# Two layers of cross-attention on one core: values four units back inside the query projection, scores after six steps, and more low parts on VectorE

## The reference

```python
# layer 0: grouped attention, 32 query heads of 32, 8 key/value heads
q = x @ Wq + bq;  k = ctx @ Wk + bk;  v = ctx @ Wv + bv
attn = softmax(q k^T / sqrt(32) + mask)
out = (attn v) @ Wo + bo
x = layer_norm(out + x) * gamma + beta            # eps 1e-6
# layer 1: 16 heads of 64, keys and values from the normalised context
a = layer_norm(ctx) * gamma1 + beta1              # eps 1e-5
Q = x @ Wq1.T;  K = a @ Wk1.T;  V = a @ Wv1.T
x = x + tanh(gate) * ((softmax(where(mask, Q K^T / 8, -inf)) V) @ Wo1.T)
```

## Time and profile before

| | |
|---|---|
| Median of three runs | 1791.67 us |
| The profiled execution, its own time | 1794.66 us |
| Its span on the core | 1792.8 us |
| PE busy | 1725.7 us, 96% of the span |
| PE weight loads busy | 1432.0 us, 80% |
| VectorE busy | 1149.0 us, 64% |
| GpSimd busy | 1106.7 us, 62% |
| ScalarE busy | 582.1 us, 32% |
| DMA | 278.01 MB, 155 GB/s on average |

### The profile page before, as it was taken

One profiled execution on the slowest core, in us unless ns is written; L12 is line 12 of the kernel. 1 busy time (PEld: TensorE's weight loads), 2 busy tenths in 40 slices (PEclk: granted clock), 3 DMA queues, 4 the chain that ended last, 5 costly groups with the idle time before them and its releaser, 6 DMA issues.

```text
span 1792.8 us, 22372 instructions
## 1 busy us (share of the span) xinstructions
PE 1725.7 (96%) x8449; PEld 1432.0 (80%) x8449; DVE 1149.0 (64%) x1089; ACT 582.1 (32%) x667; POOL 1106.7 (62%) x607
## 2 busy tenths in 40 slices
PE   6899999999999799999999999999999999999998
PEld 5788887888888688888888877788888888888886
DVE  6888888888888566565656555446644664466442
ACT  4444444444445434333433323113311331133110
POOL 2677777777777857565656677436644664466331
PEclk9999999999999999999999999999999999999999
DMA  7433332323225557776777845453744464465432
GB/s 213 115 85 77 102 79 72 83 72 86 72 69 146 159 175 250 222 251 212 254 225 235 284 150 176 144 172 129 224 153 164 144 209 141 165 186 168 140 112 88
DMA packets 277487, 278.01 MB, mean 155 GB/s; under 512 B 62202, under 2 KB 230276, under 8 KB 277380
## 3 DMA queue, kind: packets, MB, share of 16 engines
q1 hardware_dynamic: 275188, 274.49, 49.9%
q10 hardware_dynamic: 2192, 2.10, 0.4%
HBM read 174.77 MB, written 101.71 MB: 154 GB/s over the span
## 4 chain that ended last, share of the span: by engine, by line
PE 58%; DVE 18%; issue 11%; POOL 7%; ACT 6%; DMA 1%; SPq 0%; POOLq 0%; DVEq 0%; ACTq 0%
PE ps L53 18%; PE ps L54 18%; PE ps L55 18%; DVE small L1059 3%; DVE pr L1079 3%; ACT pr L822 3%; DVE pT0r L1092 2%; DVE pT1r L1092 2%; DVE xT0r L990 2%; DVE xT1r L990 2%; ACT ot L816 2%; PE ps L682 1%; PE ps L690 1%; POOL xb L1339 1%; POOL y L1353 1%
## 5 line engine op out<-in xcount | busy, mean ns | idle before, releaser
L1388 POOL TENSOR_TENSOR x2Tl<-x2r,x2Th 128x1024 fp32r<-128x1024 f32 x32 | 76.8, 2400 | 291.9 <-ACT x2Th L931 291.9
L1188 DVE STREAM_TRANSPOSE x2r<-xd 128x1024 f32<-128x1024 f32 x32 | 68.8, 2150 | 211.8 <-PE ps L55 211.8
L1324 POOL TENSOR_TENSOR pr<-pr,small 128x1024 f32<-128x1024 f32 x64 | 122.8, 1919 | 105.0 <-DVE small L1085 105.0
L931 ACT CAST x2Th<-x2r 128x1024 fp32r<-128x1024 f32 x32 | 33.6, 1051 | 376.9 <-DVE x2r L1188 376.9
L1319 POOL TENSOR_TENSOR pr<-pr,small 128x1024 f32<-128x1024 f32 x64 | 123.9, 1936 | 25.5 <-DVE small L1063 25.5
L1059 DVE TENSOR_REDUCE small<-pr 128x16 f32<-128x1024 f32 x64 | 78.0, 1219 | 78.6 <-ACT pr L822 78.6
L1339 POOL TENSOR_TENSOR xb<-xb,bo 128x1024 f32<-128x1024 f32 x32 | 77.8, 2431 | 76.3 <-DMA xb<-in_x_dram 76.3
L1353 POOL TENSOR_TENSOR y<-y,bet 128x1024 f32<-128x1024 f32 x32 | 77.7, 2427 | 52.4 <-DVE y L1104 52.4
L53 PE MATMUL ps<-wo0h,oc1l 128*128 128x512 f32 x256 | 102.6, 401 | 3.6 <-DVE y L1143 3.6
L1104 DVE TENSOR_TENSOR y<-y,gam 128x1024 f32<-128x1024 f32 x32 | 54.6, 1706 | 80.0 <-ACT y L856 80.0
L53 PE MATMUL ps<-wo0h,oc0l 128*128 128x512 f32 x256 | 102.5, 401 | 2.0 <-DVE wo0l L1014 1.6
(11 more groups left out here) (370 smaller groups left out, 5473.1 us busy)
## 6 DMA issues: line engine op xcount, KB each, us to landing
o_scratch<-ot SPq DMA_DIRECT2D x256, 64.0 KB, 1.8
ocr<-o_scratch SPq DMA_DIRECT2D x16, 1024.0 KB, 7.9
xb<-in_x_dram SPq DMA_DIRECT2D x32, 512.0 KB, 6.8
x_scratch<-y SPq DMA_DIRECT2D x32, 512.0 KB, 5.3
a_scratch<-ost SPq DMA_DIRECT2D x64, 256.0 KB, 3.4
b_scratch<-ost SPq DMA_DIRECT2D x64, 256.0 KB, 5.8
xd<-x_scratch SPq DMA_DIRECT2D x128, 128.0 KB, 2.9
raw<-b_scratch SPq DMA_DIRECT2D x64, 256.0 KB, 5.6
```

The costliest lines, as they stand in the source:

```text
L1324: nc.gpsimd.tensor_tensor(heads(v), heads(v), mx.unsqueeze(2).to_broadcast([P, TPB * GRP, KEYS]), ALU.subtract)\
L1388: nc.gpsimd.tensor_tensor(x2T[1][:], x2r[:], f32(x2T[0][:]), ALU.subtract).then_inc(x2_lo, 1)
```

## The change

**First loads.** SP now issues the context, then Wk, then all four tiles of x; ScalarE issues the two small biases, waits for the context, and then issues Wv and its bias. PE turns the context before it turns the biases, and ScalarE and VectorE split the context before Wk. VectorE makes the low parts of the first four tiles of x; GpSimd made two of them.

**Attention.** In PE's slot u the order is now: four steps of the query projection, the values of unit u-4, two steps, the scores of unit u-1, two steps. ScalarE does the exponential at the head of its slot and `ot` behind the casts. The groups of Wq are split one unit earlier (`wq_groups`), SP's order inside a slot is k, Wq, x, v, and quarter 3 of Wq is issued in slot 1, not before slot 0. The parts of Wo are made one in each slot from 57 to 64. The statistics and the normalised rows of the context are made in slots 12 to 15, stored to a new scratch and loaded again in slot 60. Pieces of the first chunk of `oc` are split two units later.

**Seam.** From h = 53 the low parts of `oc` and all low parts of A of the first batch are on VectorE, and so are the eight of B, `beta` of the last tile, and the low parts of the first and the last probabilities. `coefficients` stands ahead of `residual` on GpSimd there. ScalarE issues the store of the last tile of x2. The pieces of A are loaded and split one in each slot.

```diff
         def wo_groups(u):
-            return (7,) if u == UNITS else (5, 6) if u == UNITS - 1 else (u - (UNITS - 6),) if UNITS - 6 <= u < UNITS else ()
+            return (u - (UNITS - 7),) if UNITS - 7 <= u <= UNITS else ()
+        def wq_groups(u):
+            return (2, 3) if u == 0 else (u + 3,) if u + 3 < KT else ()
...
             load_ctx(ctx, ctx_ld)
-            sp.dma_start(bv_row[:], row(w["bv0"], KV0)).then_inc(b_ld, 16)
-            sp.dma_start(wvr[:], w["Wv0"].rearrange("(k p) n -> p k n", p=P)).then_inc(kv_ld1, 16)
-            load_x(sp, 2)
-            load_x(sp, 3)
+            sp.dma_start(wkr[:], w["Wk0"].rearrange("(k p) n -> p k n", p=P)).then_inc(kv_ld0, 16)
+            for n in range(4):
+                load_x(sp, n)
...
                 if 1 <= u and u + 1 < UNITS:
                     sp.wait_ge(scores, u)
                     load_k(u + 1)
-                if 3 <= u <= UNITS:
-                    sp.wait_ge(pv, u - 2)
-                    load_v(u - 1)
+                if u == 1:
+                    load_wq(3)
...
+                if 4 <= u <= UNITS + 1:
+                    sp.wait_ge(pv, u - 3)
+                    load_v(u - 2)
```

PE's slot:

```diff
                 if u < UNITS:
                     query(range(0, 4))
+                if 4 <= u < UNITS + 4:
+                    values_of(u - 4)
+                if u < UNITS:
+                    query(range(4, 6))
                 if 1 <= u <= UNITS:
                     v = u - 1
...
                 if u < UNITS:
-                    query(range(4, KT))
+                    query(range(6, KT))
...
-                if 3 <= u < UNITS + 3:
-                    v = u - 3
```

ScalarE's and GpSimd's rows at the seam, and VectorE's row:

```diff
+            for c in range(2, 4):
+                split_ab(1, 0, c)
+            act.wait_ge(normed, NTILE)
+            act.dma_start(d["x2"][P * (NTILE - 1):, :], y[(NTILE - 1) % 3][:]).then_inc(y_st[(NTILE - 1) % 3], 16)
+            for c in range(4, KT):
                 split_ab(1, 0, c)
...
             total(1)
+            prob_lo(0)
             gamma(NTILE - 1)
-            for c in range(1, KT, 2):
+            dve.wait_ge(scaled, NTILE)
+            nc.vector.tensor_tensor(y[(NTILE - 1) % 3][:], y[(NTILE - 1) % 3][:], bet0[:], ALU.add).then_inc(normed, 1)
+            for c in range(KT):
                 low(1, 0, c)
...
             turn_prob(NTILE - 1)
+            prob_lo(NTILE - 1)
             finish(NTILE - 2)
...
-                if half == 1 and n + 1 < NTILE:
+                seam = h > LEAD + TAB * KT
+                if half == 1 and n + 1 < NTILE and not seam:
                     residual(n + 1)
...
                 if half == 1:
                     coefficients(n)
-                if later:
+                if seam and half == 1 and n + 1 < NTILE:
+                    residual(n + 1)
+                if later and not seam:
                     chunk_lo(h // 4 + 1, 1)
```

More of the change, by code:

```diff
@@ L606, in query, with values_of @@
                         last.then_inc(q_done, 1)
+                def values_of(v):
+                    pe.wait_ge(p_lo, v + 1)
+                    pe.wait_ge(v_ld[v % 2], 16 * 4 * (v // 2 + 1))
+                    after(pe, o_ev, v - 1)
+                    for c in range(2):
+                        last = three(nc, V[v % 2], [vb[v % 2][:, c, x] for x in (0, 1)], [pT[v % 2][x][:, c].rearrange("p j n -> p (j n)") for x in (0, 1)],
+                                     c == 0, c == 1)
+                    last.then_inc(pv, 1)
                 if u < UNITS:
                     query(range(0, 4))
+                if 4 <= u < UNITS + 4:
+                    values_of(u - 4)
+                if u < UNITS:
+                    query(range(4, 6))
                 if 1 <= u <= UNITS:
@@ L626, in slot @@
                     half_tile(u - UNITS)
-                if 3 <= u < UNITS + 3:
-                    v = u - 3
-                    pe.wait_ge(p_lo, v + 1)
-                    pe.wait_ge(v_ld[v % 2], 16 * 4 * (v // 2 + 1))
-                    after(pe, o_ev, v - 1)
-                    for c in range(2):
-                        last = three(nc, V[v % 2], [vb[v % 2][:, c, x] for x in (0, 1)], [pT[v % 2][x][:, c].rearrange("p j n -> p (j n)") for x in (0, 1)],
-                                     c == 0, c == 1)
-                    last.then_inc(pv, 1)
                 if 1 <= u - UNITS < 3:
@@ L1030, in vector @@
                 nc.vector.tensor_scalar(kf[:, h], V[h][:, :CTX], bk[:, h:h + 1], SCALE0, ALU.add, ALU.mult).then_inc(kfull, 1)
-            split_x(2)
-            split_x(3)
+            for n in range(4):
+                split_x(n)
             split_wq(0)
@@ L1421, in gpsimd @@
                     prepare(u - UNITS)
-            low(1, 0, 0)
-            prob_lo(0)
             scale(1)
-            beta(NTILE - 1)
-            for c in (2, 4, 6):
-                low(1, 0, c)
             for u in range(2, NTILE):
```

181 lines of the change are left out of this document (96 added, 85 removed).

## The result

The changed kernel takes 1772.82 us (median, 1771.54 to 1774.79), the kernel before 1791.12 (four executions each). The ratio is 0.9897, with a 95% interval of 0.9884 to 0.9909: 18.3 us less, a little over half of what was forecast, and 2.8 above the upper end of the range.

The account below looks back on a forecast made before the run. PE was taken as the bound, busy 1725.7 of 1792.8 us, with waits to remove. Terms -2.3 + 3.3 - 15 - 10.4 - 10.5 - 0.4 = -35.3 from 1791.67 gave 1756.4 us; range 1749 to 1770.

Parts of the forecast that it names:

- Attention: From 116.01 to 580.08, taking `ot` out of the softmax cycle makes PE the bound; -15 us, bounds -18 and 0.
- the ring: Attention's cycle without PE matmuls of projection: pT transpose, cast, `ot`, exponential, sum, turned tile, mask, maximum; 17.13 us a pair, then 16.2.
- All 18 come back, less the norm of the context: Attention: 27 pairs at 16.52 make 446.0 against 464.07; 18 us return, less 2 to 3 for the norm.
- Front: Before unit 0: context lands at 6.0, first unit starts at 31.1 instead of 33.45; -2.3 us.
- First units: To unit 8: k's 5.98 wait goes, a 6.9 wait comes from group 4's cast awaiting quarter 2; +3.3 us.
- 17.9 after the start: First units: quarter 2 of Wq lands 17.9 us after PE's first unit starts, issued 11.7 after it.
- End of the attention: From 585.78 to 622.04, 13.7 us are lost; reordered half tiles and shorter chains return -10.4 us, bounds -12 and -5.
- What stays: End of the attention: the 1.6 us wait for the last query's low part, and as much for Wo's last group.
- Seam: Between the layers: the 3.64 wait with its lower clock returns 6.1 us, earlier logits 4.4; -10.5 us.
- Rival (b): Low parts on VectorE collide with GpSimd in front and seam, each 2.1 us and not 1.15; +12.4, 1768.8 us; chance 0.10.
- End: Last low part and tile 30's finish on VectorE, 1.15 + 0.71 for GpSimd's 2.34; -0.4 us, bounds 0 and -2.
- Rival (a): Attention: the softmax cycle is not what holds it, units stay at 17.1, the 15 are gone; 1773.4 us; chance 0.15.

Follow-up runs that it names:

- e4_ot: The changed kernel with ScalarE's copy of the attention output (`ot`) back ahead of the exponential, as before the change; 1789.81 us.
- e1_norm: The changed kernel with the context norm's statistics, coefficients and rows spread over slots 11 to 22, and chunk 0's four pieces in slots 28 to 40; 1761.65 us.
- e8_front: e7_wt with Wk's load waiting for the context, Wv's behind it on SyncE, both split in halves, two low parts of x on GpSimd; 1748.59 us.
- e11_split: e7_wt with Wk and Wv split in halves and the low parts of x's first two tiles on GpSimd, load order kept; 1751.95 us.
- e16_halves: e7_wt with Wq's low part at the end of VectorE's slots, Wk and Wv split in halves, all low parts of x on VectorE; 1747.29 us.
- e2_wq: The changed kernel with Wq's column groups split as before the change (slot u splits group u + 2); 1764.64 us.
- e7_wt: The changed kernel with the edits of e1_norm and e2_wq, plus Wk1's first transposition on VectorE ahead of the multiplication by gamma; 1748.97 us.
- e9_seam: The changed kernel with the seam's lines of the change undone on all engines; 1779.13 us.
- e15_rows: The changed kernel with only the context norm's two rows on ScalarE moved from ahead of slot 16's exponential to behind it; 1769.69 us.

## Why the prediction was wrong

The direction and most of the mechanisms were right. Of the 16.4 us that it was off by the medians, 12.4 lie in terms of the sum (22.9 measured between marks, 35.3 forecast). The rest is that the sum was worked out from a profiled execution 3.0 above its median and taken from the median, and that the changed kernel's lies 0.8 below its own. By its own steps:

- **Attention, -15 forecast, -6.8 measured: the step that failed most.** The mechanism is shown: `ot` in the ring by e4_ot, and TensorE's 16.52 as the bound by e1_norm, whose 27 pairs take the forecast 446.0. What failed is "All 18 come back, less the norm of the context", in both halves. The 18 were not all the ring's: the text took 17.13 for every pair, but 4.0 of the 18 were the chunk's four pieces, which stay and cost 3.4; the ring's share was 14.0, and e4_ot gives 14.3. And the norm, "some 2 to 3", costs 7.7. I took its pieces' lateness as absorbed in slack; but the ring gains only 0.14 us per pair on TensorE (16.38, mask to mask from 187.26 to 203.64, against 16.52), so slack eaten by one piece is not back for the next two slots later. 18.0 - 7.7 - 3.4 = 6.9, against 6.8.
- **Front, -2.3 forecast, +1.0 measured, near 0 over thirteen traces.** "I take it as landed at 6.0" failed: 7.55, and 8.5 in e8_front without Wk beside it. VectorE was done at 32.7 as its own chain has it; the later stop in this trace, V's projection, moved with Wv's load behind the context, was in no term. Taking away the sharing with GpSimd was right (e11_split against e16_halves).
- **First units, +3.3 forecast, +2.4 measured.** Right, with the named cause: the cast waits 9.80 us for quarter 2, and TensorE 4.96 where 6.9 was said. e2_wq shows that it is the order alone. "17.9 after the start" is not how it goes, though: quarter 2 is issued near 44.5 wherever unit 0 starts, and so an earlier start only makes the wait longer (6.46 in e1_norm).
- **End of the attention, -10.4 forecast, -7.6 measured.** The waits named as gone are gone. "What stays" left out that the transposition of Wk1 stands behind gamma: the projection's wait grew from 1.63 to 4.49. e7_wt takes it away.
- **Seam, -10.5 forecast, -10.5 measured.** Both named parts are there, but that the sums agree is partly luck: -6.7 to the first logits (6.1 forecast), -3.3 from there to the fourth (-4.4), and -0.5 in the tile behind it, where the clock is. The second part is short where probT0l on VectorE took 2.73 us and not 1.23, GpSimd scaling probabilities beside it until 1088.87; no run tests that. Rival (b) did not come true for B, but was hardly put to the test: its low parts are 1.13 apart, and GpSimd has no row from 1088.87 to 1106.85. e9_seam shows 6.3 (medians) to 7.4 us (traces) of the seam as the edits' own, and all of it up to the fourth logits.
- **End, -0.4 forecast, -2.3 measured:** the wait is 1.93, where 2.3 was forecast and 2.73 were waited before. The rest is that the clock stayed up (a first matmul of 0.47, 0.79 before); the bound for that was -2.

Rival (a) would have given 1773.4, almost the time measured, and is wrong: pairs do take 16.5. A total that fits does not speak for its mechanism. The range was too narrow: the attention's own bound of 0 would give 1771.4, the norm had no bound of its own, and the chunk stood in no term.

## What to carry to other kernels

Before the time that a stage loses is counted as coming back, list it round by round. Here 18 us over 27 pairs were taken as one cause; nineteen pairs of 17.1 and four of 18.1 show two, and the edit removed one of them. Work that is added beside the new bound (here the norm) has to be priced piece by piece, against slack that may refill by a tenth of a microsecond per round. Put such pieces where the row of their own engine shows idle time behind the urgent instruction; the same 2.4 us of work cost 3.8 ahead of an exponential (e15_rows), and nothing that shows where e1_norm has it. Read each in-order engine's row for what stands ahead of what others wait for: a cast that waits for a late load, a transposition behind a normalisation.

## What the runs showed of the hardware

- Subtractions shared between VectorE and GpSimd gained nothing: two on VectorE beside two on GpSimd took 5.33 us (e11_split), four on VectorE alone 5.01 (e16_halves), and two after GpSimd's were done 2.35 (e8_front).
- A stall early in the stage that TensorE bounds stays in the time: lateness of -7.2 at unit 8 was -7.1 at unit 62, 457 us later (e2_wq).
- After TensorE's wait of 4.44 us its first matmul took 0.79 and the tile to the next logits 24.0 us, after one of 3.03 0.50 and 21.9; in the steady part it is 21.76. In the sixteen other traces the wait at this place is 3.65 to 5.69 us, and the tile takes 23.2 to 24.8.
- The context landed at 7.55 with Wk issued right behind it, at 10.2 with Wv too and the bias row of V issued at once, and at 8.5 with that bias row but neither Wk nor Wv. Why it is not sooner then stays open; no run moved the bias row by itself.
